# A third PSUM bank for the exponential scores: the step sums go through the work ring, and x's transpositions move to slots 8 to 11

## The chip, the cores and the metric

The kernel runs on one core of one Trainium2 chip. The metric is the device time of one execution in microseconds; the time given for a kernel is the median of its runs.

## What is computed

x is (16, 512, 512) in float32: 16 batches of 512 tokens with 512 features. The reference runs two attention layers one after the other, and the change touches the first only. With the masks all ones it computes, for each batch and each of H = 16 heads of 32 features:

```
xn  = layer_norm(x, norm_w, norm_b)
q   = (xn @ q_w + q_b).reshape(B, T, H, -1)
k   = (xn @ k_w + k_b).reshape(B, T, H, -1)
att = softmax(einsum('bnhl,bmhl->bnmh', q, k) + (1 - mask) * -1e6, axis=2)
v   = ((xn @ v_w + v_b) * src_mask[:, :, None]).reshape(B, T, H, -1)
y   = einsum('bnmh,bmhl->bnhl', att, v).reshape(B, T, D)
e   = silu(cond) @ emb_w + emb_b          # scale and shift, from the condition
h   = silu(layer_norm(y, ...) * (1 + scale) + shift) @ out_w + out_b
x   = x + h
```

The second layer is an efficient-attention block with 8 heads, of the same sizes.

## The kernel before

The program has two phases. `attention_phase` computes q, k, v, the softmax numerators and y of the first layer for all batches, and leaves y and the softmax sums in DRAM. `projection_phase` does the rest. Only `attention_phase` changes.

**Steps and slots.** A batch b is done in NG = 4 steps g, and a step handles a group of HG = 4 heads. A step has SLOTS = 16 slots, k = 0 to 15, written out by hand in the program of each engine. In the slots of step (b, g), TensorE (PE) does four kinds of work:

- *Exponential scores* (`exp_scores`, L521 [PE]): one 512-column matmul each, 16 in a step, called e0 to e15 here. They lag by LAG = 3 slots: slot k computes exponential score k - 3 of this step (slots 0 to 2 do e13 to e15 of the step before). ScalarE (ACT) turns each into `probs` (`exp`, L745). There are two `exp_bank`s, so score e must wait until ACT has read score e - 2.
- *Maximum scores* (`max_scores`, L506): the same scores of the next step, transposed, m0 to m15, one and a half in a slot, in slots 0 to 10. Even slots have one; odd slots have two, with a quarter of a projection between them. VectorE (DVE) takes the row maxima (`maximum`, L879) from two `max_bank`s: score m waits until maximum m - 2 is done.
- *Bursts*: in the slot of e6 (slot 9) `weigh_values` of the previous step's key tiles 2 and 3 (L532, 16 records), then `sum_probs` (L546), which sums `probs_sum` over the keys; in the slot of e8 (slot 11) `weigh_values` of this step's key tiles 0 and 1. `probs_sum` is added up by GpSimd (POOL, `add_probs`, L284, three adds of 128x2048 in a step); the last batch's last step does it on DVE.
- *Work through the ring* of two `work_bank`s, taken in turn in a fixed order (`uses_of`): the projections of q in slots 0 to 3 and of k in slots 4 to 7 for two steps ahead (L489, three matmuls in a quarter, one quarter in a slot), two tiles of v in steps 0 and 3 in slots 8 to 11 and 13 to 15, the turned maxima `m` in slot 12 (`transpose_max`, L512), and in step 1 the four transpositions of x of the next batch (`transpose_x`, L496) in slots 8, 9, 11 and 13. A use takes its bank when the use two before it has been read (`take_bank`). For q and k the bank is read by ACT (`high_of`, L719) and then by DVE (`low_of`, L865). For x it is ACT `high_of_x` (L713) and DVE `low_of_x` (L860), the latter one slot later. For v it is DVE `add_value_bias` (L874) in slot 11 or 15. For m it is DVE `split_shift` (L890, L892), which SP then sends by two DMAs (`shift_rows`, L333) into the rows that e0 of the next step needs.

ACT also issues the DMAs of the high parts of q and k behind `high_of` (`stack_high`, L726), copies y (`copy_y`, L752) at e6, and in step 0 copies the sums of the batch before (`copy_sums`, L758) at e8. DVE also normalises the next x in slots 5 to 8 of step 1 (`normalise_x`, L854, a tensor_scalar from SBUF to SBUF), takes its statistics in slot 13 of step 0, and in batch 0 runs `finish_film` there (L970 to L1003).

**The sums.** `sum_probs` accumulates the four steps of a batch in one bank, `sums_bank`, which PE clears at g = 0. All eight banks are in use: 2 for maxima, 2 for exponentials, 1 for y, 1 for the sums, 2 for the ring.

## Time and profile before

| what | value |
|---|---|
| median of 3 runs | 2814.29 us (2809.64 to 2818.85) |
| time of the profiled execution | 2816.7 us |
| its span, first to last instruction | 2814.9 us |
| mean granted TensorE clock | 0.981 of full |
| attention_phase, to the last sums' store | about 1565 us |
| busy: PE, DVE, ACT, POOL | 95%, 65%, 44%, 48% |
| one full batch, in the steady state | 92.0 us |

A batch's length is read from the timeline: the same instruction (the turned maxima of step 2) starts at 708.73 us, at 800.75 us and at 892.78 us. Fifteen batches (0 to 14) have this form; batch 15 has no q, k or x of a next batch. The page gives the shares of each engine; the timeline lists instructions in order of time, with the idle time before one and what released it in brackets.

### The profile page before, as it was taken

How to read it: one execution, taken by the hardware profiler on the slowest of the kernel's cores; microseconds unless marked ns; L12 is line 12 of the kernel's file. 1: busy time of each engine (PE TensorE's matmuls, PEld its weight loads, DVE VectorE, ACT ScalarE, POOL GpSimd, SP SyncE). 2: the span in 40 equal slices, each digit the busy share in tenths (PEclk: the TensorE clock that was granted, in tenths of full speed). 3: DMA queues.
4: the chain of work that ended last, by engine and by line, in shares of the span. 5: the costliest groups of instructions: out<-in, count | busy, mean ns of one | idle time of the engine just before them, and what ended most of it. 6: DMA issues, size and time to landing. Idle time of an engine off the chain costs nothing. (4 is left out here: it accounts for less than half of the span.)

```text
span 2814.9 us, 43874 instructions
## 1 busy us (share of the span) xinstructions
PE 2676.0 (95%) x13890; PEld 1951.0 (69%) x13890; DVE 1823.3 (65%) x3276; ACT 1226.6 (44%) x2040; POOL 1343.4 (48%) x598
## 2 busy tenths in 40 slices
PE   6999999999999999999999689999999999999997
PEld 3566666656665666666664478888888888888886
DVE  4666666666666665666664666666777667766673
ACT  2455555555555555555555323333333333333332
POOL 0366656566656656665666234334333333333332
PEclk9999999999999999999998799999999999999999
DMA  7556656665666566656653411111111111111100
GB/s 182 124 96 96 101 78 97 99 100 78 97 100 99 79 96 98 95 81 94 95 80 58 147 35 50 49 49 49 49 45 49 45 40 42 41 49 44 39 30 31
DMA packets 114915, 211.44 MB, mean 75 GB/s; under 512 B 12408, under 2 KB 14508, under 8 KB 114876
## 3 DMA queue, kind: packets, MB, share of 16 engines
q1 hardware_dynamic: 78012, 143.81, 22.1%
q10 hardware_dynamic: 36864, 67.13, 17.9%
q8 instruction: 22, 0.36, 0.1%
q14 instruction: 17, 0.14, 0.0%
HBM read 74.87 MB, written 34.18 MB: 39 GB/s over the span
## 5 line engine op out<-in xcount | busy, mean ns | idle before, releaser
L879 DVE TENSOR_REDUCE negmax<-max_bank 128x1 f32<-128x512 f32 x1024 | 681.4, 687 | 311.3 <-PE max_bank L506 309.6
L745 ACT ACTIVATE probs<-exp_bank 128x512 f32<-128x512 f32 x1024 | 587.1, 596 | 530.6 <-PE exp_bank L521 494.5
L284 POOL TENSOR_TENSOR probs_sum<-probs_sum,probs 128x2048 f32<-128x2048 f32 x126 | 580.7, 4609 | 78.9 <-ACT probs L745 74.7
L284 POOL TENSOR_TENSOR probs_sum<-probs 128x2048 f32<-128x2048 f32 x63 | 287.7, 4567 | 571.3 <-ACT probs L745 571.3
L506 PE MATMUL max_bank<-k_stack,q_stack 98*128 98x512 f32 x1024 | 423.0, 417 | 22.7 <-DVE negmax L879 18.3
L521 PE MATMUL exp_bank<-q_stack,k_stack 100*128 100x512 f32 x1024 | 422.6, 424 | 22.4 <-ACT probs L745 21.7
L506 PEld LDWEIGHTS max_bank<-k_stack,q_stack 98*128 98x128 f32 x1024 | 193.7, 191 | 140.5 <-issue 58.8
L521 PEld LDWEIGHTS exp_bank<-q_stack,k_stack 100*128 100x128 f32 x1024 | 193.5, 190 | 128.1 <-ACT probs L745 72.8
L1500 POOL TENSOR_TENSOR sT_lo<-silu,sT_hi 128x512 fp32r<-128x512 f32 x128 | 172.9, 1371 | 176.4 <-DVE sT_hi L1615 176.4
L532 PE MATMUL y_bank<-probs,v_sb 128*32 128x512 f32 x2048 | 251.0, 608 | 0.0
L1281 PE MATMUL b_work<-ident,area 128*128 128x128 f32 x1536 | 192.9, 280 | 24.9 <-DMA b_sums<-sums_scratch 13.2
L1255 PE MATMUL b_work<-b_wout_hi,sT_hi 128*128 128x512 f32 x512 | 201.7, 394 | 9.6 <-issue 5.1
L1281 PEld LDWEIGHTS b_work<-ident,area 128*128 128x128 f32 x1536 | 176.1, 145 | 39.1 <-DMA b_sums<-sums_scratch 14.1
L1255 PE MATMUL b_work<-b_wout_lo,sT_hi 128*128 128x512 f32 x512 | 200.9, 392 | 0.0
L1255 PE MATMUL b_work<-b_wout_hi,sT_lo 128*128 128x512 f32 x512 | 200.9, 392 | 0.0
L1495 POOL TENSOR_TENSOR rstd_y<-var_eps_y,b_minus_half 128x4 f32<-128x4 f32 x32 | 32.7, 1022 | 333.2 <-DVE var_eps_y L1579 333.2
L1615 DVE CAST sT_hi<-silu 128x512 fp32r<-128x512 f32 x128 | 102.2, 819 | 103.8 <-ACT silu L1440 103.7
L1479 ACT ACTIVATE area<-area 128x512 f32<-128x512 f32 x64 | 40.4, 632 | 274.6 <-POOL area L1545 274.6
L1440 ACT ACTIVATE silu<-b_work,film_b,film_a 128x512 f32<-128x512 f32 x128 | 93.0, 776 | 129.0 <-PE b_work L1281 101.5
L874 DVE TENSOR_TENSOR v_sb<-work_bank,v_bias 128x512 f32<-128x512 f32 x64 | 44.2, 691 | 153.7 <-PE work_bank L489 153.7
L1515 POOL TENSOR_TENSOR result<-area,row_out 128x512 f32<-128x512 f32 x64 | 83.0, 1307 | 125.8 <-DMA out_x<-result 125.8
L532 PEld LDWEIGHTS y_bank<-probs,v_sb 128*32 128x32 f32 x2048 | 53.9, 110 | 124.0 <-issue 109.7
(203 smaller groups left out, 5294.8 us busy)
## 6 DMA issues: line engine op xcount, KB each, us to landing
q_stack<-q_stage ACTq DMA_DIRECT2D x128, 256.0 KB
k_stack<-k_stage ACTq DMA_DIRECT2D x128, 256.0 KB
x_sb<-in_x SPq DMA_DIRECT2D x16, 1024.0 KB, 5.7
q_stack<-q_stage SPq DMA_DIRECT2D x64, 256.0 KB
k_stack<-k_stage SPq DMA_DIRECT2D x64, 256.0 KB
yT_scratch<-y_stage SPq DMA_DIRECT2D x64, 256.0 KB
area<-yT_scratch SPq DMA_DIRECT2D x16, 1024.0 KB, 5.2
area<-in_x SPq DMA_DIRECT2D x64, 256.0 KB, 2.8
```

The source lines that it names most:

```text
L284: eng.tensor_tensor(probs_sum[:, :, :], so_far, probs[:, mt, :, :], ALU.add).then_inc(probs_added, 1)
L506: pe.matmul(max_bank[m % 2][:, :], q_stack[0:ROWS_MAX, g, j, nt * P:(nt + 1) * P], k_stack[0:ROWS_MAX, g, j, :], start=True, stop=True).th ...
L521: pe.matmul(exp_bank[k % 2][:, :], k_stack[0:ROWS_EXP, g, j, mt * P:(mt + 1) * P], q_stack[0:ROWS_EXP, g, j, :], start=True, stop=True).th ...
L532: last = pe.matmul(y_bank[DH0 * j:DH0 * (j + 1), :], v_sb[:, mt, P * j + DH0 * g:P * j + DH0 * (g + 1)], probs[:, mt, j, :], start=(mt == ...
L745: act.activation(probs[:, mt, j, :], exp_bank[k % 2][:, :], ACT.Exp).then_inc(exp_done, 1)
L879: dve.tensor_reduce(negmax[:, m:m + 1], max_bank[m % 2][:, :], AXX, ALU.max, negate=True).then_inc(max_done, 1)
L1255: last = pe.matmul(out, lhs(a, kt), rhs(c, kt), start=(kt == 0 and a + c == 0), stop=(kt == KT - 1 and a == 1))
L1281: last = pe.transpose(out[:, i * P:(i + 1) * P], src(i), ident[:, :])
L1440: act.activation(silu[:, kt % SILUS, :], bank(u), ACT.Silu, scale=film_columns(film_a[film], kt, row), bias=film_columns(film_b[film], kt, ...
L1500: pool.tensor_tensor(sT_lo[:, kt, :], silu[:, kt % SILUS, :], sT_hi[:, kt, :].bitcast(F32), ALU.subtract).then_inc(sT_lo_done, 1)
L1515: pool.tensor_tensor(result[:, tt, :], x_sb[:, tt, :], rows["out1"][:, :], ALU.add).then_inc(result_biased, 1)
L1615: dve.tensor_copy(sT_hi[:, kt, :], silu[:, kt % SILUS, :]).then_inc(sT_hi_done, 1)
```

## The change

- `sums_bank` goes. Its PSUM bank becomes `exp_bank[2]`. Exponential score e uses bank e mod 3, except e15, which uses bank 1. So e2 to e14 wait for the reading of e - 3 (e2: e14 of the step before), e15 waits for e13, e1 waits for e15 of the step before, and e0 for e12 of the step before.
- `sum_probs` of every step takes a bank of the ring, as a use `s` in slot 9, and no longer accumulates. DVE adds each step's sum into `sums_stage` in SBUF (`gather_sums`, slot 9): a copy at g = 0, an add at the other steps. ACT's `copy_sums` goes.
- The first tile of v takes its quarters in slots 9, 10, 10, 11. x is transposed in slots 8, 9, 10 and 11, so all before `m`. The ring's order in step 1 was q, k, x0, x1, x2, m, x3; it becomes q, k, x0, s, x1, x2, x3, m. In steps 0 and 3 it was q, k, v, m, v'; it becomes q, k, s, v, m, v'. A batch has 24 uses where it had 20.
- DVE takes only the first maximum of a slot at the slot's start; the second comes at the slot's end, behind the slot's other DVE work.
- `finish_film` moves from slot 13 to slot 4 of the very first step. The film products use `exp_bank[2]` and `y_bank` in place of `sums_bank`.

```diff
@@ -169,9 +169,8 @@
         minus_half = sb("minus_half", [P, TT])
 
         max_bank = [bank(f"max_bank{i}") for i in range(2)]
-        exp_bank = [bank(f"exp_bank{i}") for i in range(2)]
+        exp_bank = [bank(f"exp_bank{i}") for i in range(3)]
         y_bank = bank("y_bank")
-        sums_bank = bank("sums_bank")
         work_bank = [bank(f"work_bank{i}") for i in range(2)]
 
...
         def uses_of(g, last):
-            u = []
+            at = []
             if not last or g < NG - 2:
-                u += ["q", "k"]
-            if g == 0:
-                u += ["v2"]
+                at += [(QUARTERS[n][0], n) for n in "qk"]
+            if g == 0 or (g == NG - 1 and not last):
+                mt = 2 if g == 0 else 0
+                at += [(QUARTERS["v"][0], f"v{mt}"), (QUARTERS["v'"][0], f"v{mt + 1}")]
             if g == 1 and not last:
-                u += [f"x{tt}" for tt in range(TT - 1)]
-            if g == NG - 1 and not last:
-                u += ["v0"]
+                at += [(k, f"x{tt}") for tt, k in enumerate(X_TURNS)]
             if not last or g < NG - 1:
-                u += ["m"]
-            if g == 1 and not last:
-                u += [f"x{TT - 1}"]
-            if g == 0:
-                u += ["v3"]
-            if g == NG - 1 and not last:
-                u += ["v1"]
-            return u
+                at.append((MAX_TURN, "m"))
+            return [n for _, n in sorted(at + [(LAG + FIRST_BURST, "s")])]
+
+        QUARTERS = {"q": (0, 1, 2, 3), "k": (4, 5, 6, 7), "v": (9, 10, 10, 11), "v'": (13, 14, 15, 15)}
+        X_TURNS = (8, 9, 10, 11)
+        MAX_TURN = 12
+        FIRST_BURST = 6
+        SECOND_BURST = 8
 
         FIRST_USES = [f"x{tt}" for tt in range(TT)] + ["q0", "k0", "q1", "k1", "m", "v0", "v1"]
         USES = sum(len(uses_of(g, False)) for g in range(NG))
         assert USES % 2 == 0
 
 
-        QUARTERS = {"q": (0, 1, 2, 3), "k": (4, 5, 6, 7), "v": (8, 9, 10, 11), "v'": (13, 14, 15, 15)}
-        X_TURNS = (8, 9, 11, 13)
-        MAX_TURN = 12
-
...
         def use(b, g, what, last=False):
 
-            n = len(FIRST_USES) + sum(len(uses_of(h, last)) for h in range(g)) + uses_of(g, last).index(what)
+            uses = uses_of(g, last)
+            n = len(FIRST_USES) - 1 + sum(len(uses_of(h, last)) for h in range(g)) + uses.index(what)
+            if type(b) is int and b == 0 and g == 0 and uses.index(what) < uses.index("s"):
+                n += 1
             return n, b * USES + n
+
+        def final_use():
+
+            n = len(FIRST_USES) - 1 + sum(len(uses_of(h, True)) for h in range(NG))
+            return n, (B - 1) * USES + n
+
+        def exp_bank_of(k):
+            return exp_bank[1 if k == SLOTS - 1 else k % 3]
+
+        def exps_in_front(s, k):
+
+            if k < 3:
+                return SLOTS * (s - 1) + (13, 16, 15)[k]
+            return SLOTS * s + (k - 1 if k == SLOTS - 1 else k - 2)
 
...
-        def add_probs(eng, s, mt, first=False):
+        def add_probs(eng, s, mt, sums_use=None):
 
             eng.wait_ge(exp_done, SLOTS * s + HG * (mt + 1))
             if mt == 1:
-                if not first:
-
-                    eng.wait_ge(sums_full, s)
+                if sums_use is not None:
+
+                    eng.wait_ge(work_full, sums_use + 1)
                 so_far = probs[:, 0, :, :]
...
                     pe.wait_ge(shift_in[g], 2 * DMA * (b + 1))
-                if not (first and k < 2):
-                    pe.wait_ge(exp_done, SLOTS * step_of(b, g) + k - 1)
-                pe.matmul(exp_bank[k % 2][:, :], k_stack[0:ROWS_EXP, g, j, mt * P:(mt + 1) * P],
+                if not (first and k < 3):
+                    pe.wait_ge(exp_done, exps_in_front(step_of(b, g), k))
+                pe.matmul(exp_bank_of(k)[:, :], k_stack[0:ROWS_EXP, g, j, mt * P:(mt + 1) * P],
                           q_stack[0:ROWS_EXP, g, j, :], start=True, stop=True).then_inc(exp_full, 1)
...
                     pe.wait_ge(y_read, s)
+                if type(s) is int and s == 0:
+                    pe.wait_ge(film_step, 2)
...
-            def sum_probs(b, g):
-
-                s = step_of(b, g)
-                pe.wait_ge(probs_added, (TT - 1) * (s + 1))
-                if type(s) is int and s == 0:
-                    pe.wait_ge(film_step, 2)
-                if g == 0 and not (type(b) is int and b == 0):
-                    pe.wait_ge(sums_read, b)
+            def sum_probs(b, g, number):
+
+                out = take_bank(number)
+                pe.wait_ge(probs_added, (TT - 1) * (step_of(b, g) + 1))
                 for j in range(HG):
-                    last = pe.matmul(sums_bank[DH0 * j:DH0 * (j + 1), :], head_sel[:, g, :],
-                                     probs_sum[:, j, :], start=(g == 0), stop=(g == NG - 1))
-                last.then_inc(sums_full, 1)
+                    last = pe.matmul(out[DH0 * j:DH0 * (j + 1), :], head_sel[:, g, :],
+                                     probs_sum[:, j, :], start=True, stop=True)
+                last.then_inc(work_full, 1)
...
-                if e == 6 and not first:
+                if e == FIRST_BURST and not first:
                     weigh_values(*before, 2)
                     weigh_values(*before, 3)
-                    sum_probs(*before)
-                if e == 8:
+                    sum_probs(*before, use(b, g, "s", last))
+                if e == SECOND_BURST:
                     weigh_values(b, g, 0)
                     weigh_values(b, g, 1)
...
-            def copy_sums(b):
-                act.wait_ge(sums_full, NG * (b + 1))
-                if not (type(b) is int and b == 0):
-                    act.wait_ge(sums_stored, DMA * HG * b)
-                act.activation(sums_stage[:, :], sums_bank[:, :], ACT.Copy).then_inc(sums_read, 1)
...
-                if e == 8 and g == 0 and not first:
-                    copy_sums(b - 1)
...
+            def gather_sums(b, g, sums_use, sums_use_in_front):
+
+                static, number = sums_use
+                dve.wait_ge(work_full, number + 1)
+                if g == 0:
+                    if not (type(b) is int and b == 0):
+                        dve.wait_ge(sums_stored, DMA * HG * b)
+                    done = dve.tensor_copy(sums_stage[:, :], work_bank[static % 2][:, :])
+                else:
+                    dve.wait_ge(work_read, sums_use_in_front + 1)
+                    done = dve.tensor_tensor(sums_stage[:, :], work_bank[static % 2][:, :], sums_stage[:, :], ALU.add)
+                done.then_inc(work_read, 1)
...
                     if has_next:
-                        for m in maxima(k):
+                        for m in maxima(k)[:1]:
                             maximum(n_b, n_g, m)
...
+                    if k == LAG + FIRST_BURST and not (type(b) is int and b == 0 and g == 0):
+                        before = (b, g - 1) if g else (b - 1, NG - 1)
+                        in_front = None if g == 1 else use(b, g - 1, "s", last)[1] if g else use(b - 1, NG - 1, "s")[1]
+                        gather_sums(*before, use(b, g, "s", last), in_front)
...
                     if g == 0 and not last and k == 13:
                         statistics_of_x(b + 1)
-                        if type(b) is int and b == 0:
-                            finish_film()
+                    if type(b) is int and b == 0 and g == 0 and k == 4:
+                        finish_film()
+                    if has_next:
+                        for m in maxima(k)[1:]:
+                            maximum(n_b, n_g, m)
...
-                add_probs(dve, step_of(B - 1, NG - 1), mt)
+                add_probs(dve, step_of(B - 1, NG - 1), mt, use(B - 1, NG - 1, "s", True)[1])
+            gather_sums(B - 1, NG - 1, final_use(), use(B - 1, NG - 1, "s", True)[1])
```

## Rows read from the trace of the kernel before

**Rows 1.** The page, busy time of the engines.

```profile
PE 2676.0 (95%) x13890; PEld 1951.0 (69%) x13890; DVE 1823.3 (65%) x3276; ACT 1226.6 (44%) x2040; POOL 1343.4 (48%) x598
```

**Rows 2.** Waits, us in total, times, longest, 100 to 1600 us.

```profile
PEld exp_bank L521 <- ACT probs L745: 72.5, 144, 1.2
...
PE exp_bank L521 <- ACT probs L745: 21.7, 54, 0.8
...
PE work_bank L496 <- DVE xT_lo L860: 12.7, 15, 0.9
```

**Rows 3.** Timeline of PE, end of step 2 (start, length, instruction, idle before).

```profile
800.78 0.48 PE L521 MATMUL exp_bank<-q_stack,k_stack 100*128 100x512 f32 x1
801.60 0.98 PE L521 MATMUL exp_bank<-q_stack,k_stack 100*128 100x512 f32 x2 [0.34 <-ACT probs L745]
802.78 0.50 PE L521 MATMUL exp_bank<-q_stack,k_stack 100*128 100x512 f32 x1 [0.21 <-ACT probs L745]
```

**Rows 4.** Timeline of ACT, the same stretch.

```profile
800.95 2.97 ACT L745 ACTIVATE probs<-exp_bank 128x512 f32<-128x512 f32 x5 [1.54 <-PE exp_bank L521]
```

**Rows 5.** Timeline of PE and its weight loads around e3, slot 6 of step 2.

```profile
882.13 0.39 PE L506 MATMUL max_bank<-k_stack,q_stack 98*128 98x512 f32 x1
...
882.45 0.19 PEld L521 LDWEIGHTS exp_bank<-q_stack,k_stack 100*128 100x128 f32 x1 [0.36 <-ACT probs L745]
```

**Rows 6.** Timeline of DVE, slots 5 to 8 of step 1.

```profile
859.04 1.39 DVE L879 TENSOR_REDUCE negmax<-max_bank 128x1 f32<-128x512 f32 x2
860.35 0.97 DVE L854 TENSOR_SCALAR x_sb<-x_sb,mv,rstd 128x512 f32<-128x512 f32 x1
...
861.84 0.53 DVE L854 TENSOR_SCALAR x_sb<-x_sb,mv,rstd 128x512 f32<-128x512 f32 x1
```

**Rows 7.** Timeline of POOL, the same stretch.

```profile
856.43 4.61 POOL L284 TENSOR_TENSOR probs_sum<-probs_sum,probs 128x2048 f32<-128x2048 f32 x1
```

**Rows 8.** Timeline of PE, slots 8 to 15 of step 1.

```profile
863.03 0.50 PE L506 MATMUL max_bank<-k_stack,q_stack 98*128 98x512 f32 x1 [0.31 <-DVE negmax L879]
...
866.85 0.50 PE L506 MATMUL max_bank<-k_stack,q_stack 98*128 98x512 f32 x1
...
870.64 0.66 PE L496 MATMUL work_bank<-ident,x_sb 128*128 128x128 f32 x4
...
872.72 0.66 PE L496 MATMUL work_bank<-ident,x_sb 128*128 128x128 f32 x4 [0.84 <-DVE xT_lo L860]
...
874.55 0.50 PE L521 MATMUL exp_bank<-q_stack,k_stack 100*128 100x512 f32 x1 [0.71 <-ACT probs L745]
```

**Rows 9.** Timeline of DVE and ACT, slots 9 to 12 of step 1.

```profile
867.38 1.36 DVE L879 TENSOR_REDUCE negmax<-max_bank 128x1 f32<-128x512 f32 x2 [1.64 <-PE max_bank L506]
868.66 0.68 DVE L860 TENSOR_TENSOR xT_lo<-work_bank,xT_hi 128x512 fp32r<-128x512 f32 x1
...
871.34 0.60 ACT L713 ACTIVATE xT_hi<-work_bank 128x512 fp32r<-128x512 f32 x1 [1.69 <-PE work_bank L496]
871.83 1.08 ACT L745 ACTIVATE probs<-exp_bank 128x512 f32<-128x512 f32 x2
```

**Rows 10.** Timeline around finish_film in batch 0: DVE, POOL, PE.

```profile
109.75 3.21 DVE L995 TENSOR_SCALAR film_a<-film_a 128x64 f32<-128x64 f32 x2
...
108.16 4.60 POOL L284 TENSOR_TENSOR probs_sum<-probs_sum,probs 128x2048 f32<-128x2048 f32 x1 [1.34 <-ACT probs L745]
...
115.28 0.49 PE L506 MATMUL max_bank<-k_stack,q_stack 98*128 98x512 f32 x1 [3.17 <-DVE negmax L879]
```

**Rows 11.** Stretch by stretch: us, busy (count) of PE, PEld, DVE, ACT, POOL, granted clock, DMA, GB/s.

```profile
803.10:812.50 9.40, 9.40 (x41) 7.40 (x41) 7.28 (x11) 4.99 (x9) 9.03 (x2) 1.00 0.69 175
110.00:120.00 10.00, 6.68 (x21) 4.77 (x21) 7.82 (x14) 2.89 (x5) 6.83 (x4) 0.83 0.00 0
1243.00:1247.00 4.00, 4.00 (x12) 3.18 (x13) 1.38 (x2) 1.38 (x3) 4.00 (x1) 0.60 0.03 6
```

**Rows 12.** The instructions of L333, the DMAs of the shift rows.

```profile
DMA to landing us min/median/max: 1.8/1.9/4.6
```

More of the change, by code:

```diff
@@ L382, in step @@
                 if g == 0 and not first:
-                    store_sums(b - 1)
+                    store_sums(b - 1, use(b, 0, "s", last)[1])
                 if not last or g < NG - 1:
@@ L398, in store_y, with store_sums @@
                 sp.dma_start(yT_dram[b].rearrange("(j g l) t -> g j l t", j=HG, g=NG)[g], y_stage[:, g % 2, :]).then_inc(y_stored[g % 2], DMA)
-            def store_sums(b):
-                sp.wait_ge(sums_read, b + 1)
+            def store_sums(b, sums_use):
+                sp.wait_ge(work_read, sums_use + 1)
                 for j in range(HG):
@@ L418, in _ @@
             store_y(B - 1, NG - 1)
-            store_sums(B - 1)
+            store_sums(B - 1, final_use()[1])
             for i in range(2):
@@ L445, in step @@
                     return
-                add_probs(pool, s, 1, first)
+                add_probs(pool, s, 1, None if first else use(b, g, "s", last)[1])
                 add_probs(pool, s, 2)
@@ L560, in film_products @@
                 pe.wait_ge(emb_in, DMA * 4 * (i + 1))
-                for half, out in enumerate((sums_bank, y_bank)):
+                for half, out in enumerate((exp_bank[2], y_bank)):
                     for c in range(CT // HG):
@@ L571, in film_columns @@
                 for dt in range(TE // P):
-                    last = pe.matmul((exp_bank[1], sums_bank)[i][:, dt * B:(dt + 1) * B],
+                    last = pe.matmul((exp_bank[1], y_bank)[i][:, dt * B:(dt + 1) * B],
                                      film_rows.rearrange("p h n -> p (h n)")[:, dt * P:(dt + 1) * P], row_sel[:, :],
@@ L639, in _, with exp_slot @@
             pe.wait_ge(ones_in, 2 * DMA)
-            def exp_slot(b, g, e, first=False):
+            def exp_slot(b, g, e, first=False, last=False):
                 exp_scores(b, g, e, first)
                 before = (b, g - 1) if g else (b - 1, NG - 1)
-                if e == 6 and not first:
+                if e == FIRST_BURST and not first:
                     weigh_values(*before, 2)
                     weigh_values(*before, 3)
-                    sum_probs(*before)
-                if e == 8:
+                    sum_probs(*before, use(b, g, "s", last))
+                if e == SECOND_BURST:
                     weigh_values(b, g, 0)
@@ L658, in step @@
                     if not (first and g == 0 and k < LAG):
-                        exp_slot(*exp_of(b, g, k), first and g == 0)
+                        exp_slot(*exp_of(b, g, k), first and g == 0, last)
                     if first and g == 0 and k == LAG:
@@ L705, in _ @@
             weigh_values(B - 1, NG - 1, 3)
-            sum_probs(B - 1, NG - 1)
+            sum_probs(B - 1, NG - 1, final_use())
         @block.scalar
@@ L744, in exp @@
                     act.wait_ge(probs_added, (TT - 1) * (s - 1) + max(mt, 1))
-                act.activation(probs[:, mt, j, :], exp_bank[k % 2][:, :], ACT.Exp).then_inc(exp_done, 1)
+                act.activation(probs[:, mt, j, :], exp_bank_of(k)[:, :], ACT.Exp).then_inc(exp_done, 1)
             def copy_y(b, g):
@@ L765, in copy_film @@
                 act.wait_ge(film_full, i + 1)
-                for half, src in enumerate((sums_bank, y_bank)):
+                for half, src in enumerate((exp_bank[2], y_bank)):
                     act.activation(film_rows[:, half, :], src[:, :], ACT.Copy).then_inc(film_copied, 1)
@@ L794, in exp_slot @@
                 exp(b, g, e, first)
-                if e == 6 and not first:
+                if e == FIRST_BURST and not first:
                     copy_y(*((b, g - 1) if g else (b - 1, NG - 1)))
-                if e == 8 and g == 0 and not first:
-                    copy_sums(b - 1)
             def step(b, g, last=False, first=False):
@@ L832, in _ @@
             copy_y(B - 1, NG - 1)
-            copy_sums(B - 1)
         @block.vector
@@ L968, in add_film_bias @@
                 dve.wait_ge(film_made, i + 1)
-                e = (exp_bank[1], sums_bank)[i][:, 0:2 * KT * B].rearrange("p (c b) -> p c b", b=B)
+                e = (exp_bank[1], y_bank)[i][:, 0:2 * KT * B].rearrange("p (c b) -> p c b", b=B)
                 dve.tensor_tensor(film_a[i][:, :, :], e[:, 0:KT, :], by_row(shared.eb[i][:, 0:KT]), ALU.add)
```

2 lines of the change are left out of this document (1 added, 1 removed).

## The prediction

> **What bounds the kernel now.** I read the page first. PE is busy for 95% of the span, the other engines for 44 to 65% [rows 1]. So the gain can only be idle time of PE, and the price can only be new idle time of PE. The table of waits says what that idle time is [rows 2]: PE waits for ACT to read an exponential bank (21.7 us, and its weight loads 72.5 us more, much of that hidden under a matmul that still runs), and for the low part of x (12.7 us); waits for maxima are of the same size. Then I went through the timeline of one full batch, 92.0 us, and marked each place where one matmul starts later behind the last than the usual 0.23 us (41 in 9.4 us in dense slots, a gap of 0.2 among them) [rows 11]. Four kinds of place were left that the change touches: the end of step 2, slot 6 of every step, slots 5 to 15 of step 1, and the very first step. In the dense slots (q, k, v quarters) the exponentials come 1.2 us apart, ACT needs 0.6 us for one, and a third bank has nothing to do there.
>
> **End of step 2: the third bank pays.** Slots 12 to 15 and slot 0 hold nothing but exponentials. e10 starts on PE at 800.78; e11 can't start before e9 is read and starts at 801.60; e13 waits for e11 and starts at 802.78 [rows 3]. ACT starts e9 at 800.95 and takes 2.97 us for five, 0.6 each, because it is itself fed in turn from two banks [rows 4]. Two that are both ready follow one another in 0.48 us (two in 1.08, one 0.6) [rows 9]. With three banks e11 follows e10 at once; e12 waits for e9 (read at 801.55, start 801.60); e13 waits for e10 (read at 800.95 + 0.48 + 0.60 = 802.03, start 802.10). That is 802.78 - 802.10 = 0.68 us saved. e15 and e1 still wait for the score two before, but they lie in slots 2 and 4, which are dense. Steps 0 and 3 fill slots 13 to 15 with v and have no such wait.
>
> **Slot 6.** ACT issues the two DMAs of q behind slot 3, so e1 is read late and e3 waits: its weight load 0.36 us, and the matmul starts 0.32 us after m8 instead of 0.23, and the next one 0.1 late behind it [rows 5]. In the batch that I went through, all four steps have this; the 144 waits of the weight loads [rows 2] are enough for it in all. With three banks e3 waits for e0, which is long read. That is 0.2 us a step. DVE is nearly as late there (m9 waits for maximum 7), so I take 0.18. In step 1 DVE is late anyway (below), and I take nothing. A batch gains 3 x 0.18 = 0.54.
>
> **Step 1, slots 5 to 8: the new order on DVE costs.** Before, DVE does maxima 7 and 8, then normalises the first tile of x: 0.97 us from 860.35, to 861.32, against 0.53 for the next one [rows 6]. POOL's add runs from 856.43 to 861.04 [rows 7]. The normalisation seems to stand until POOL has finished. The first step shows the same larger: two tiny operations of L995 take 3.21 us and end at 112.96, POOL's add ends at 112.76 [rows 10]. Maximum 7 starts at 859.04, and two operations of DVE follow one another in 0.6 us; the change puts the normalisation ahead of maximum 8, at about 859.64. It still ends at 861.32, and maximum 8 comes behind it, at about 861.24 to 861.92. m10 needs it; PE would be there about 1 us earlier (two slots, ten matmuls, before m12 without its wait) and starts at 861.98. DVE then has maximum 9 (to 862.5), a normalisation (to 862.97), maximum 10 (to 863.58), and m12 starts at 863.64, where it was 863.03 [rows 8]: +0.61. Two readings are to be weighed here. If the 0.97 us is a fixed cost of a first normalisation, the move costs nothing, DVE's sum up to maximum 10 is what it was, and m12 stays at 863.03. If it is a wait for POOL, it costs the 0.61. Both long rows end 0.2 to 0.3 us behind an add of POOL, so I take the wait. The Trainium skill (SBUF — State Buffer, "Who interferes with whom") says that VectorE's tensor_scalar in its two-port mode and a GpSimd instruction exclude each other for a whole instruction. By that rule the sum is the one below, and without it the sum would be 15 x 0.61 = 9 us lower; this case's rows agree with it (0.97 against 0.53).
>
> **Step 1, slots 9 to 15.** Before, x3 waits for the low part of x2 (0.84 us idle, start 872.72), and e13 for ACT (0.71, start 874.55); from m13 at 866.85 to e13 it is 7.70 us [rows 8]. In the new ring order x1 follows s, and its bank was x0's. x0's low part is computed by DVE behind maximum 13, and m13 comes behind the burst. Maximum 13 starts 0.53 after m13, the low part 0.6 later, takes 0.68 [rows 9], and x1 starts just after: m13 + 1.84, where before x1 came right behind m13, 0.33 after it. So there is 1.5 us of new idle time. m14, e7, m15, x2, e8 and the burst follow at their distances of before, in a sum of 2.0, and x3 1.85 behind the burst (no wait now: x1 was read during it): m13 + 5.69. ACT starts x3's high part 0.70 later and e9 0.49 behind that (871.34 against 870.64; 871.83) [rows 9], and reads it in 0.6, so e12 starts at x3 + 1.85 and e13, 0.48 later, at x3 + 2.33: m13 + 8.02. That is +0.32. A small wait of e6 goes (-0.08). Step 1 costs 0.61 + 0.32 - 0.08 = +0.85.
>
> **What I cost at nothing, with its cover.** The 64 gathers take DVE some 0.68 us each, by the nearest row, an operation with one PSUM and one SBUF operand [rows 9], 44 us in all. They lie behind maximum 13 and delay only maximum 14, which nobody waits for before m0 of the next step; DVE stood idle for 1.64 us before maximum 13 [rows 9]. Without that cover, 0.6 us a step or 38 us. The sum's matmuls are as many as before. The wait of s for a ring bank was met long before in steps 0, 2 and 3 (q was read in slot 4); in step 1 it needs k's low part, about 0.5 us ahead. Behind s on PE stand m13 and all maxima, so a lack there would show at once. ACT loses 16 copies of 0.6 us, out of idle time. SP sends the sums' four DMAs two slots earlier, so shift_rows has a free queue. In step 1 DVE now does x3's low part ahead of the shift: the two DMAs are issued at about 875.7 and 876.3, behind x3's low part at 875.1, and land 1.9 us later at 878.2 [rows 12]; e0 is due three dense slots behind e13 (875.4 + 3.8), its weights at 879.0. That is 0.8 us to spare; at the longest landing, 4.6, e0 would wait 1.9 us, once in a while.
>
> **First step.** finish_film now runs when POOL is idle. Before it left PE idle for 3.17 us [rows 10], and over 10 us around it the granted clock was 0.83, which is 1.7 us lost at 1.2 instead of 2.4 GHz [rows 11]. Without the wait for POOL (2.9 of the 3.21 us) some 1.7 us of small operations are left; in slot 4 they hold up m9 by about 1.5. Net -3.4 (bounds 0 and -4.9).
>
> **The sum.** Fifteen batches: 15 x (-0.68 - 0.54 + 0.85) = -5.6. Batch 15 has no x, so its step 1 ends like step 2, and has slot 6 with a DMA of q twice: -0.68 - 0.36 = -1.0. First step -3.4. Together -10.0 us: 2816.7 becomes 2806.7 for the profiled execution. That execution was 2.4 us above the median of 2814.3, so the median goes to 2804.3.
>
> **Rivals.** (a) *Likeliest, 0.43*: the sum, 2804, own range 2796 to 2811. (b) *Step 1 costs nothing, 0.22*: the normalisation doesn't stand behind POOL and x1's wait only replaces the waits of x3 and e13 that go. Then 15 x (-0.68 - 0.54 - 0.08) - 4.4 = -24: 2790. For it: two waits, 0.84 and 0.71, do go. Against it: rows 6 and 7. (c) *The exponential banks are not what slot 6 waits for, 0.20*: DVE, busy without a break there, holds m9 at the same time, and 15 x 0.54 + 0.36 = 8.5 us stay away: 2813, no change. For it: maxima and exponentials are equally late there. (d) *The clock, the other side, 0.15*: after the end of step 1, once in the trace, the granted clock falls to 0.60 over 4 us, and 1.6 us are lost [rows 11]. That was behind the waits of 0.84 and 0.71. If the new waits in step 1 (1.0 before m10, 1.5 before x1) bring this in every batch, it is +24 - 10 = +14: 2828. It decides from about 12 of the 15 batches on. Against it: the old waits did it only once in fifteen, and the new ones lie among more matmuls. The Trainium skill (TensorE: Matmul & The Clock Gate, "HAM oscillation") says that pauses between bursts of matmuls bring the array back to its lower clock; the trace agrees for that one place, and the rule gives (d) its place among the rivals.
>
> **Range and chances.** A measurement here tells about 0.3%, 8.4 us, from no change. Of (a) some six in ten lie beyond that bound. Faster 0.26 + 0.22 = 0.48; same 0.17 + 0.18 = 0.35; slower 0.15 + 0.02 = 0.17. The range from 2786 to 2823 holds (a), (c), most of (b) and the nearest part of (d).
>
> **What the changed profile would show.** Right: the idle time of PE <- ACT at the end of step 2 shrinks to about 0.3 us, no wait of a weight load before e3, a wait of about 1.5 us of x1 for xT_lo, none of x3, a normalisation of about 1.6 us in slot 5, m10 waiting for a maximum; L995 at some 0.2 us each; a batch of 91.6 us. Wrong: a normalisation of 0.53 us there (then (b)); e3 gaps still 0.32 with m9 waiting (c); a granted clock under 1 in the dense slots of step 2 (d); a wait of s or e0 that I cost at nothing.

## The result: 0.17% slower, and the profile after

The changed kernel takes 2819.69 us (median of 12 runs, 2817.21 to 2825.5), the kernel before 2814.74 us on the same chips (12 runs); the ratio is 1.0017, 95% interval 1.0009 to 1.0024. The forecast was 2804.3: the time moved the other way. It lies inside the stated range of 2786 to 2823, but that range is wide because it takes in rivals, and in the main the cause is none of them. In a later set of runs it came out the same: 2820.31 against 2815.11, ratio 1.0014 (1.0005 to 1.0023). The profiled span is 2818.6 us, 3.7 more than before.

The length of a batch says where to look. I take the distance between the same instruction in neighbouring batches (the first copy of the turned maxima, in slot 12), as the median of eight batches in the middle:

| us from slot 12 to slot 12 | step 3 to 0 | 0 to 1 | 1 to 2 | 2 to 3 | batch |
|---|---|---|---|---|---|
| before | 24.50 | 24.19 | 20.52 | 22.82 | 92.03 |
| after | 24.39 | 26.71 | 18.85 | 22.81 | 92.76 |

(The copy waits for other work of DVE in step 1, so the two middle columns are to be read together: 44.71 before, 45.56 after.) The batch was forecast 0.37 us shorter and is 0.73 longer. Step 1 costs +0.85, about as forecast (these two columns also hold slot 6 of step 2, which became 0.09 shorter, so step 1 by itself costs 0.9). What is missing is the gain of the third bank: the column that holds the end of step 2 stands at 22.81, and of slot 6 little more than 0.1 us can be seen, in the column from step 3 to step 0.

The page after: busy time of the engines, to be read beside [rows 1].

```profile
PE 2668.5 (95%) x13890; PEld 1944.4 (69%) x13890; DVE 1859.3 (66%) x3340; ACT 1201.3 (43%) x2024; POOL 1344.5 (48%) x598
```

The 64 gathers are there on DVE (its busy time rose by 36 us in all), and ACT's 16 copies are gone. The table of waits of the changed kernel, 100 to 1600 us, answers to [rows 2]:

```profile
PEld exp_bank L532 <- ACT probs L754: 36.4, 76, 0.8
...
PE work_bank L507 <- DVE xT_lo L860: 20.8, 15, 1.5
...
PE max_bank L517 <- DVE negmax L892: 18.3, 35, 1.5
...
PE max_bank L517 <- DMA k_stack<-k_stage: 7.5, 15, 0.5
PE exp_bank L532 <- ACT probs L754: 6.6, 18, 0.5
```

PE waits for ACT 15.1 us less, and its weight loads 36.1 us less. In their place stand 8.1 us more for x's low part, some 5 us more for maxima (12.9 before), and a line that the kernel before did not have among PE's waits: 15 waits of 0.5 us, one in each batch, for the rows of k.

**The end of step 2**, timeline of PE and ACT after, answering to [rows 3] and [rows 4]:

```profile
897.18 0.27 PE L523 MATMUL work_bank<-ident,negmax 128*16 128x128 f32 x1
897.21 1.81 PE L532 MATMUL exp_bank<-q_stack,k_stack 100*128 100x512 f32 x4
899.54 0.49 PE L517 MATMUL max_bank<-k_stack,q_stack 98*128 98x512 f32 x1 [0.53 <-DMA k_stack<-k_stage]
...
897.38 2.56 ACT L754 ACTIVATE probs<-exp_bank 128x512 f32<-128x512 f32 x5 [1.53 <-PE exp_bank L532]
```

The same in the kernel before:

```profile
892.78 0.28 PE L512 MATMUL work_bank<-ident,negmax 128*16 128x128 f32 x1
...
895.16 0.39 PE L506 MATMUL max_bank<-k_stack,q_stack 98*128 98x512 f32 x1
```

e10 to e13 are one run of four now, with no wait among them that the row shows: in the steady batches e13 starts 1.31 us behind e10, where it was 2.01. ACT takes 2.56 us for the five exponentials, where it took 2.97. But m0, the first maximum score of the next step, stands 0.53 us for k's rows and starts at 899.54, 2.36 us behind the turned maxima. Before, it started 2.38 us behind them. All that the third bank saves there is given back at once. m0 needs six large DMAs of 256 KB (high part of q twice, of k twice, low part of each), and they are issued in step 2 itself. The timeline of ACT's queue and of SP's shows the first and the last issue after, and the first issue before:

```profile
884.97 1.21 ACTq L735 DMA_DIRECT2D q_stack<-q_stage  x2
...
891.70 0.61 SPq L338 DMA_DIRECT2D k_stack<-k_stage  x1
```

```profile
880.48 1.21 ACTq L726 DMA_DIRECT2D q_stack<-q_stage  x2
```

and the stretch from the first issue to m0 (columns as in [rows 11]):

```profile
885.00:899.50 14.50, 13.60 (x74) 6.67 (x72) 9.00 (x16) 7.79 (x15) 8.50 (x2) 1.00 0.89 118
```

The 16 DMA engines are 89% busy in it. The last DMA is issued 7.8 us before m0 starts, while 8 KB rows land in 1.9 us [rows 12]; that it lies in a queue behind the others is a reading that an experiment below bears out. Before the change m0 started 14.68 us behind the first issue; after it, 14.57. The semaphore events of the traces have the landing itself: the last of the six lands 14.4 us behind the first issue in both kernels (median of eleven batches). Before the change m0 started 0.28 us behind that landing without waiting for it; after the change it starts 0.12 us behind it, as soon as it can. So there was room for 0.16 us and no more: the DMAs had been just hidden by e13's wait for ACT.

**Step 1**, DVE and POOL after, answering to [rows 6] and [rows 7]:

```profile
862.62 0.68 DVE L892 TENSOR_REDUCE negmax<-max_bank 128x1 f32<-128x512 f32 x1
863.22 1.65 DVE L854 TENSOR_SCALAR x_sb<-x_sb,mv,rstd 128x512 f32<-128x512 f32 x1
864.80 1.27 DVE L892 TENSOR_REDUCE negmax<-max_bank 128x1 f32<-128x512 f32 x2
...
859.98 4.62 POOL L295 TENSOR_TENSOR probs_sum<-probs_sum,probs 128x2048 f32<-128x2048 f32 x1
```

The first normalisation takes 1.65 us; it ends at 864.87, 0.27 us behind POOL's add (859.98 + 4.62 = 864.60), the same distance as before. The timeline of PE, answering to [rows 8], and of DVE, answering to [rows 9]:

```profile
865.53 0.50 PE L517 MATMUL max_bank<-k_stack,q_stack 98*128 98x512 f32 x1 [0.74 <-DVE negmax L892]
...
872.88 0.66 PE L507 MATMUL work_bank<-ident,x_sb 128*128 128x128 f32 x4 [1.38 <-DVE xT_lo L860]
...
871.54 0.69 DVE L892 TENSOR_REDUCE negmax<-max_bank 128x1 f32<-128x512 f32 x1 [1.65 <-PE max_bank L517]
872.14 0.68 DVE L860 TENSOR_TENSOR xT_lo<-work_bank,xT_hi 128x512 fp32r<-128x512 f32 x1
872.74 0.68 DVE L884 COPY sums_stage<-work_bank 128x512 f32<-128x512 f32 x1
```

m10 waits 0.74 us for maximum 8. x1 waits 1.38 us: DVE idles for 1.65 us, does maximum 13, and only then x0's low part, which x1 needs. x3 waits no more.

**The first step.** finish_film after, answering to [rows 10], and the stretches, answering to [rows 11]:

```profile
97.54 0.30 DVE L1008 TENSOR_SCALAR film_a<-film_a 128x64 f32<-128x64 f32 x2
...
99.55 0.50 PE L517 MATMUL max_bank<-k_stack,q_stack 98*128 98x512 f32 x1 [1.49 <-DVE negmax L892]
```

```profile
92.00:102.00 10.00, 8.51 (x46) 6.91 (x44) 7.09 (x19) 3.48 (x6) 0.00 (x0) 1.00 0.66 124
110.00:120.00 10.00, 9.79 (x42) 7.83 (x42) 8.46 (x20) 6.41 (x11) 7.74 (x5) 1.00 0.02 5
```

The 3.21 us have become 0.30, PE idles 1.49 us, and the granted clock is 1.00 in both places.

### The profile page after: what moved, and what is told of

Read it like the earlier page. It is cut to its first block and busy times, and to the rows that moved or that the text cites. A ratio compares the mean times of both kernels' runs of the same rounds, so it can differ in the third digit from the quotient of the medians.

```text
span 2818.6 us, 44156 instructions
## 1 busy us (share of the span) xinstructions
PE 2668.5 (95%) x13890; PEld 1944.4 (69%) x13890; DVE 1859.3 (66%) x3340; ACT 1201.3 (43%) x2024; POOL 1344.5 (48%) x598
## 3 DMA queue, kind: packets, MB, share of 16 engines
q10 hardware_dynamic: 36864, 67.13, 17.5%
## 5 line engine op out<-in xcount | busy, mean ns | idle before, releaser
L754 ACT ACTIVATE probs<-exp_bank 128x512 f32<-128x512 f32 x1024 | 573.1, 598 | 552.0 <-PE exp_bank L532 468.9
L517 PE MATMUL max_bank<-k_stack,q_stack 98*128 98x512 f32 x1024 | 430.0, 424 | 36.6 <-DVE negmax L892 23.6
L532 PE MATMUL exp_bank<-q_stack,k_stack 100*128 100x512 f32 x1024 | 411.2, 416 | 8.8 <-ACT probs L754 6.6
```

Source lines behind the costliest of these rows:

```text
L517: pe.matmul(max_bank[m % 2][:, :], q_stack[0:ROWS_MAX, g, j, nt * P:(nt + 1) * P], k_stack[0:ROWS_MAX, g, j, :], start=True, stop=True).th ...
L532: pe.matmul(exp_bank_of(k)[:, :], k_stack[0:ROWS_EXP, g, j, mt * P:(mt + 1) * P], q_stack[0:ROWS_EXP, g, j, :], start=True, stop=True).the ...
L754: act.activation(probs[:, mt, j, :], exp_bank_of(k)[:, :], ACT.Exp).then_inc(exp_done, 1)
```

## Experiments

There are eleven, and each time is the median of 4 to 12 runs of the kernel. Its ratio is to runs of the kernel before on the same chip, whose medians lie between 2815.1 and 2816.8. Where a median of the changed kernel is needed, it is 2820.3, from its own repeat. The batch lengths are read as in the table above.

### Two banks for the exponentials in the changed kernel

```diff
-            return exp_bank[1 if k == SLOTS - 1 else k % 3]
+            return exp_bank[k % 2]
...
-            if k < 3:
-                return SLOTS * (s - 1) + (13, 16, 15)[k]
-            return SLOTS * s + (k - 1 if k == SLOTS - 1 else k - 2)
+            return SLOTS * s + k - 1
...
-                if not (first and k < 3):
+                if not (first and k < 2):
```

> The changed kernel with everything in place, but the exponential scores use two banks again (score e waits for e - 2), the third stands idle. Theory A (the third bank is worth its place only where no DMA stands behind it): at the end of step 2 nothing is lost, since the first maximum score of the next step waits for the rows of k anyway; at the end of step 1 e11 to e13 come 0.6 us later, and slot 6 costs 0.1 us more in each step: 15 x (0.6 + 0.4) = +15 us over the changed kernel, 2835. Theory B (the bank pays as predicted at the end of step 2 too): 0.68 more in each batch, +25 us, 2845. Theory C (the bank is worth nothing): 2820.

2833.15 us, ratio to the kernel before 1.0062 (1.0048 to 1.0075); a batch of 93.64, 0.88 more than the changed kernel. The columns: 24.48, 26.71, 19.62, 22.83. All of the loss but 0.1 is in the column of the end of step 1 (1 to 2, +0.77); in that of the end of step 2 it is 0.02. Theory A, with 0.88 us where it had 1.0. The bank is worth 0.9 us a batch, and nothing at the place for which I had priced it highest. Without it the wait of m0 for the rows of k is gone from the table of PE's waits: it is hidden again.

### DVE's order of before, but for slot 9

```diff
-                        for m in maxima(k)[:1]:
+                        for m in maxima(k)[:1] if k == 9 else maxima(k):
...
-                    if has_next:
+                    if has_next and k == 9:
                         for m in maxima(k)[1:]:
```

> The changed kernel with DVE's order of before in slots 0 to 8 and 10 (both maxima first, then the normalisation); slot 9 keeps the new order. Theory A (the normalisation stands behind POOL's add and carries maximum 8 with it): it takes 0.9 to 1.0 us again instead of 1.65, m10 waits no more, m12 waits 0.3 as before; 0.6 to 0.7 us less in each of 15 batches, -10 us against the changed kernel, 2810. Theory B (the long normalisation is a fixed cost of the first one, wherever it stands): no change, 2820.

2809.07 us, ratio 0.9973 (0.9964 to 0.9982); a batch of 92.13, 0.63 less than the changed kernel. DVE in slots 5 and 6 of step 1, and POOL beside it:

```profile
855.54 1.40 DVE L892 TENSOR_REDUCE negmax<-max_bank 128x1 f32<-128x512 f32 x2
856.86 0.96 DVE L854 TENSOR_SCALAR x_sb<-x_sb,mv,rstd 128x512 f32<-128x512 f32 x1
...
852.92 4.61 POOL L295 TENSOR_TENSOR probs_sum<-probs_sum,probs 128x2048 f32<-128x2048 f32 x1
```

The same instruction takes 1.65 us at one place and 0.96 at the other, and what stays is its end, 0.29 us behind POOL's add here (857.82 and 857.53). A fixed cost would not do that. Theory A.

### The low part of x0 ahead of maximum 13

```diff
+                    if g == 1 and not last and k == 9:
+                        low_of_x(0, use(b, 1, "x0")[0], high_count(b, 1, 2))
                     if has_next:
                         for m in maxima(k)[:1]:
                             maximum(n_b, n_g, m)
...
-                    if g == 1 and not last and k - 1 in X_TURNS:
+                    if g == 1 and not last and k - 1 in X_TURNS[1:]:
```

> The changed kernel with the low part of x0 ahead of maximum 13 on DVE in slot 9 of step 1, in the time in which DVE stands idle for 1.65 us. Theory A (x1's wait is one for the place of this operation in DVE's order): x1's idle time of 1.38 us goes, x2 waits some 0.3 us for the gathered sum, e13 comes about 1.2 us earlier; 15 x 1.2 = -18 us, 2802. Theory B (the time is bound by ACT's and DVE's work on the four tiles, and comes back as waits of x2, x3 or e12): less than -5 us, 2815 to 2820.

2800.13 us, ratio 0.9945 (0.9932 to 0.9959); a batch of 91.59, 1.17 less than the changed kernel, where 1.2 was expected. DVE and PE in slots 9 and 10 of step 1:

```profile
860.55 0.69 DVE L860 TENSOR_TENSOR xT_lo<-work_bank,xT_hi 128x512 fp32r<-128x512 f32 x1
862.15 0.69 DVE L892 TENSOR_REDUCE negmax<-max_bank 128x1 f32<-128x512 f32 x1 [0.91 <-PE max_bank L517]
862.75 0.68 DVE L884 COPY sums_stage<-work_bank 128x512 f32<-128x512 f32 x1
...
861.61 0.50 PE L517 MATMUL max_bank<-k_stack,q_stack 98*128 98x512 f32 x1
861.95 0.60 PE L507 MATMUL work_bank<-ident,x_sb 128*128 128x128 f32 x4
```

x1 is back right behind m13 (0.34 us). DVE does the low part in its idle time, which shrinks from 1.65 to 0.91. Theory A.

### One of the six DMAs made small, after the change and before it

```diff
-                    act.dma_start(stack_rows(what, row, g), stage[what][:, 0, :].bitcast(F32)).then_inc(stack_in[g], DMA)
+                    dst, src = stack_rows(what, row, g), stage[what][:, 0, :].bitcast(F32)
+                    if part and what == "q" and row == 2:
+                        dst, src = dst[:, 0, :], src[0:DH0, :]
+                    act.dma_start(dst, src).then_inc(stack_in[g], DMA)
```

`part` is true from batch 1 on.

> The changed kernel, in which one of the six large DMAs of a step's q and k rows (the second copy of q's high part) carries only one of the four heads from batch 1 on; the other heads keep the rows of an earlier batch, so this leaves out part of the data. Theory A (from slot 3 of step 2 on the six DMAs, one behind the other, set when m0 of the next step can start): the wait of m0 for the k rows, 0.53 us, goes, and e13 sets the start again; with it the 0.68 us of the third bank is seen: 0.5 to 0.8 us in 14 batches, -7 to -11 us, 2810. Theory B (m0's wait only hides another one, of ACT or DVE): no change, 2820.

> The kernel before, with the same shortened DMA (the second copy of q's high part carries one of four heads from batch 1 on, so part of the data is left out). Theory A (before the change, the rows of k had landed just when e13, held up by ACT, was through: the DMAs were hidden, and so was what they would do to a third bank): no change, 2816. Theory B (the DMAs slow other work down in either kernel, and the gain of the changed kernel with the short DMA was not that of m0's wait): -8 to -12 us here too, 2806.

After the change: 2804.11 us, ratio 0.9958 (0.9944 to 0.9971); a batch of 91.95, 0.81 less, of which 0.78 is in the column from step 2 to step 3 (22.03). Before the change: 2815.56 us, ratio 1.0001 (0.9991 to 1.0012), a batch of 92.07. The end of step 2 with the small DMA, after the change:

```profile
890.21 0.27 PE L523 MATMUL work_bank<-ident,negmax 128*16 128x128 f32 x1
890.24 1.81 PE L532 MATMUL exp_bank<-q_stack,k_stack 100*128 100x512 f32 x4
891.88 0.40 PE L517 MATMUL max_bank<-k_stack,q_stack 98*128 98x512 f32 x1
```

m0 starts 1.67 us behind the turned maxima, 0.69 sooner than with all six DMAs in full. That is the 0.68 us that the prediction had worked out for the third bank. The last landing comes 1.0 us sooner in both kernels (13.4 us behind the first issue). The same shortening is worth nothing before the change, so the DMAs are not slowing other work down. Theory A in both. The median fell by 16 us where 14 to 15 batches of 0.81 are some 12. In the profiled executions the largest other difference lies in one place, from slot 12 of step 1 to slot 12 of step 2 in batch 15, where PE has no projections: the changed kernel takes 22.0 us for it, this one 16.8, and the stretches show why. First the changed kernel's, then this one's:

```profile
1523.00:1545.00 22.00, 20.85 (x75) 8.38 (x73) 11.86 (x20) 9.74 (x18) 13.66 (x4) 0.69 0.10 25
```

```profile
1510.00:1527.00 17.00, 15.90 (x76) 6.21 (x74) 11.43 (x19) 9.60 (x17) 13.89 (x4) 1.00 0.09 26
```

The granted clock is 0.69 in one and 1.00 in the other. The kernel before with the small DMA has the short form too (17.5 us, where the kernel before has 21.8), and its median is no lower. The changed kernel itself has 22.0 in one profile and 20.9 in the other. So this is not shown to be an effect of the DMA; what sets it stays open.

### Both mends of step 1 together

The two edits above in one kernel.

> The changed kernel with both mends of step 1: DVE's order of before in slots 0 to 8 and 10, and the low part of x0 ahead of maximum 13 in slot 9. Theory A (two separate costs): their gains add up, 0.63 + 1.17 = 1.8 us in each of 15 batches, a batch of 90.96 us, -27 us against the changed kernel, about 2793. Theory B (one hides the other, as with the DMAs at the end of step 2): a batch of 91.4 or more, 2800.

2795.62 us, ratio 0.9933 (0.9919 to 0.9947); a batch of 91.03, 1.73 less than the changed kernel against 1.80 for the sum of the two. Two separate costs. This kernel, with the third bank and both mends, has a batch 1.0 us shorter than the kernel before.

### The first tile of v one slot earlier

```diff
-        QUARTERS = {..., "v": (9, 10, 10, 11), "v'": (13, 14, 15, 15)}
+        QUARTERS = {..., "v": (9, 9, 10, 10), "v'": (13, 14, 15, 15)}
```

> The kernel of the run before it, with the four quarters of the first tile of v in slots 9, 9, 10, 10 in place of 9, 10, 10, 11, so that DVE reads v's bank during the second burst. Theory A (the second tile of v waits in slot 13 only for that reading): the idle time of 0.33 us, with its start 0.57 us late, goes in steps 3 and 0, about 1.0 us in a batch, -15 us against the run before it. Theory B (e10 or the turned maxima hold slot 13 up at the same time): less than 0.3 us in a batch, -4 us.

2776.93 us, ratio 0.987 (0.9853 to 0.9887), the fastest kernel here: 1.3% under the kernel before, and 18.7 us under the one without this edit, where 15 x 0.86 are 13. Its profile has the short form of the stretch in batch 15 (17.9 us against 22.0). A batch of 90.17, 0.86 less than without this edit, in the columns 3 to 0 (23.92) and 2 to 3 (22.44). The wait for v (9.8 us, 31 times, both in the kernel before and in the changed one) is gone. That it is faster by more than its batches may lie in that stretch; this is not shown. In its table of PE's waits the rows of k stand with 7.4 us, much the same as the 7.5 of the changed kernel:

```profile
PE max_bank L517 <- DVE negmax L892: 12.4, 36, 1.5
PE max_bank L517 <- DMA k_stack<-k_stage: 7.4, 15, 0.6
```

### finish_film alone, in the kernel before

```diff
                     if g == 0 and not last and k == 13:
                         statistics_of_x(b + 1)
-                        if type(b) is int and b == 0:
-                            finish_film()
+                    if type(b) is int and b == 0 and g == 0 and k == 4:
+                        finish_film()
```

> The kernel before with nothing but finish_film moved from slot 13 to slot 4 of the first step. Theory A (its 3.21 us were a wait for POOL's add, and the lower clock came of PE's idle time): L995 takes 0.3 us, PE stands idle for about 1.5 us instead of 3.2, the granted clock stays at 1.00; -3 us, 2813.5. Theory B (first use of this code is what takes 3 us): no change, L995 stays long.

2810.75 us, ratio 0.9986 (0.9976 to 0.9996): -4.6 us in the medians, with an interval of about -1 to -7; expected -3. The profile agrees better: from the copy of the first turned maxima to slot 12 of step 2 in batch 0 it takes 77.7 us in place of 79.5, with a fall of the granted clock in it that costs 1.5, so 3.3 us are gained. In its timeline of DVE:

```profile
95.86 0.30 DVE L995 TENSOR_SCALAR film_a<-film_a 128x64 f32<-128x64 f32 x2
```

POOL does nothing between 92 and 102 us there. The idle time of PE is 1.31 us, the granted clock 1.00. Theory A: first use of the code costs nothing that shows.

### v one slot earlier in the kernel before

```diff
-        QUARTERS = {..., "v": (8, 9, 10, 11), "v'": (13, 14, 15, 15)}
+        QUARTERS = {..., "v": (8, 9, 10, 10), "v'": (13, 14, 15, 15)}
```

> The kernel before with the first tile of v in slots 8, 9, 10, 10 in place of 8 to 11, and nothing else. Theory A (the wait in slot 13 has nothing to do with the third bank): steps 3 and 0 become 0.4 to 0.5 us shorter each, 0.9 us in a batch, -13 us, 2802. Theory B (with two exponential banks the two projection quarters in slot 10 hold e8 up, or ACT gives the gain back): less than half of that, 2810.

2811.48 us, ratio 0.9986 (0.9977 to 0.9995). The batch is 91.26, 0.77 shorter, as theory A has it, but the median fell by 3.6 us in place of 12. Neither theory has the reason. Five of the fifteen batches have the column from step 1 to 2 longer by 1.5 us (22.05 to 22.13 where the others have 20.5). Four us of one of them, behind the end of step 1, and two of the matmuls in it:

```profile
876.00:880.00 4.00, 4.00 (x11) 3.10 (x11) 1.39 (x2) 1.42 (x3) 4.00 (x1) 0.57 0.02 6
...
877.27 0.63 PE L489 MATMUL work_bank<-xT_hi,wq_lo 128*128 128x512 f32 x1
877.69 0.63 PE L521 MATMUL exp_bank<-q_stack,k_stack 100*128 100x512 f32 x1
```

The granted clock is 0.57: for most of this stretch the array runs at 1.2 GHz, and the matmuls in it start 0.42 us behind one another, where it is 0.23 at 2.4 GHz. The kernel before has one such batch, so this edit brings four more, 6 us of the 0.77 x 15 = 11.6. Another 1.0 us goes in the step of finish_film in batch 0 (30.2 us in place of 29.2). What is left, 4.4 us, is near the 4.8 by which the profiled spans differ and the 3.6 of the medians. It is no matter of one execution: the mean granted clock is 0.976 to 0.979 in all eleven runs of this kernel, and 0.979 to 0.982 in the 21 runs of the kernel before beside it.

### Two banks in the fastest kernel, and the changed kernel again

The edit of the first experiment in the kernel with both mends and v earlier; and the changed kernel itself.

> The fastest kernel so far (both mends of step 1, v one slot earlier) with two exponential banks in use and the third idle: what the third bank is worth once the rest is mended. Theory A (as in the first run of two banks: the end of step 1 and slot 6, nothing at the end of step 2): 0.9 to 1.0 us in a batch, +15 us, 2792. Theory B (with x1's wait gone, the bank matters more at the end of step 1): 1.5 or more in a batch, 2800. Theory C (nothing): 2777.

> The changed kernel once more, on the same chip as these runs. All theories: 2819 to 2822, a batch of 92.76 us.

2795.47 us, ratio 0.9927 (0.9913 to 0.994), a batch of 91.14: 18.5 us and 0.97 us a batch more than with three banks (15 x 0.97 = 14.6). Theory A in the batch. The wait for the rows of k is gone from the table of PE's waits here too. The changed kernel: 2820.31, a batch of 92.76.

## Why the prediction was wrong

**The step that failed is the end of step 2.** The prediction worked out that e13 starts 0.68 us sooner, and put these 0.68 us into the sum 15 times, 10 us in all. e13 does start sooner, by 0.70. What stands behind e13 on PE, m0 of the next step, was not followed to what it waits for. The prediction followed the shift rows to e0 (there was room, and still is), but not the six DMAs of q and k to m0. Step 2 is the shortest step, and the last of these DMAs lands 14.4 us behind the first issue. e13's wait for ACT had hidden them with 0.16 us to spare. The pair of runs with the small DMA shows it: 0.78 us in that column after the change, nothing before. The question "where a stall goes, what is late next" has its answer here, and I asked it only of one of the two queues.

**Slot 6** is the term that was mis-sized: forecast at 0.18 us in three steps, 0.54 in all, it brought 0.1 net. PE and its weight loads there, after:

```profile
886.63 0.40 PE L517 MATMUL max_bank<-k_stack,q_stack 98*128 98x512 f32 x1
886.86 0.40 PE L532 MATMUL exp_bank<-q_stack,k_stack 100*128 100x512 f32 x1
887.10 0.49 PE L517 MATMUL max_bank<-k_stack,q_stack 98*128 98x512 f32 x1
...
887.09 0.19 PEld L517 LDWEIGHTS max_bank<-k_stack,q_stack 98*128 98x128 f32 x1 [0.27 <-DVE negmax L892]
```

e3 follows m8 by 0.23 us and m9 follows e3 by 0.24, so m9 does come 0.19 us sooner (it was 0.32 and 0.34). But now the weight load of m9 waits for DVE, and m10 comes 1.26 us behind m9 in place of 1.17: half is lost at once. That DVE is the next limit there had been rival (c), and about half of it is true. What is left, 0.1 us, can be seen whole in step 0 alone. In step 2 it lies ahead of the wait for the DMAs, which swallows it. In step 3, m8 comes 7.33 us behind m0 in place of 7.25 (with the small DMA it is 7.25 again), and the column shows nothing.

These two terms make up the miss in a batch. The forecast was -0.37 and the result +0.73, 1.10 more: 0.67 of the 0.68 at the end of step 2 and 0.43 of the 0.54 in slot 6.

**Step 1** was right in its mechanisms and nearly in its size: +0.85 forecast, +0.85 measured in the two columns, 0.9 without the 0.09 of slot 6 that they hold. Of its parts, the normalisation was forecast at 0.61 and is 0.63 (second run); x1's idle time was forecast at 1.5 and is 1.38; what was called a wait for POOL rather than a fixed cost is one (0.96 and 1.65 us for the same instruction, each ending 0.27 to 0.29 us behind the add). The Trainium skill's rule (SBUF — State Buffer, "Who interferes with whom") agrees with all three rows: the instruction is held up to the end of POOL's, and not slowed by a factor. That the instruction is in the two-port mode that the rule speaks of is shown by no run here.

**The first step** was right for this edit alone: 3.4 us forecast, 4.6 measured in the medians, with the forecast within the interval, and 3.3 in the profile. In the changed kernel less of it shows: from the first turned maxima to slot 12 of step 2 its two profiles are 0.6 and 1.8 us shorter than the kernel before, which with the 0.85 that step 1 costs makes 1.5 and 2.7. The gathers cost nothing, as said: the wait of PE for a ring bank behind a sum is not among its waits, and DVE does them beside work that nobody waits for.

**The sum** again, from the profiled executions. The marks are copies of the turned maxima, as in the table of batches.

| us | before | after |
|---|---|---|
| start to the first copy | 76.4 | 77.1 |
| to slot 12 of step 2, batch 0 | 79.5 | 78.9 |
| the next fourteen batches | 1291.1 | 1297.9 |
| to slot 12 of step 2, batch 15 | 91.0 | 90.9 |
| to the first matmul of the projection phase | 36.8 | 35.7 |
| projection phase | 1240.2 | 1238.0 |

The fourteen batches cost 6.9 us in place of 14 x 0.73 = 10.2. In the kernel before they hold a stretch of 1.5 us at the lower clock and a longer step 3 of batch 0 (23.5 us, 22.7 after); the rest is spread. The last row is no effect of the change, which does not touch that phase: in the thirteen profiles it takes between 1237.4 and 1240.3 us. The medians differ by 4.95 us, the spans by 3.7, where the forecast was -10.

Rival (d), the lower clock, did not come: the changed kernel has no such batch at all. Rival (b) is out by the second and third run. Of the cases with a chance, none was a DMA that becomes the bound. That the measured time lies within the range is luck: the range was drawn for (c) and (d), and neither is the cause.

**What the change holds.** The third bank is worth 0.9 to 1.0 us a batch in either setting, some 13 to 18 us. The change as made spends it on two places of DVE's order. Both can be mended, and the bank keeps its gain: with both mends the batch is 91.03 us, 1.0 less than before the change.

## What to carry to other kernels

When a wait is removed, name the next instruction on the same engine and follow every semaphore that it waits for back to its issue, DMAs above all: one that is hidden with 0.16 us to spare leaves no line in the table of waits. A fixed order on one engine has to be read against another's bank ring: the low part of x0 was ready, the engine was idle, and 1.2 us a batch hung on one maximum ahead of it. Where two places are mended at once, measure each alone: the gain of the bank was hidden here by two losses, each easy to take away.

## What the runs showed of the chip

The granted clock fell in some batches behind the end of step 1, always in kernels with x's transpositions in slots 8, 9, 11 and 13: in one of fifteen batches of the kernel before, in one of it with the small DMA, in two with only finish_film moved, and in five with v one slot earlier (0.57 over 4 us, 1.5 us lost each). There it fell in none of the nine profiles with the transpositions in slots 8 to 11, two of them with two banks. The end of step 1 has idle times of PE of 0.84 and 0.71 us close to one another, and little work between. The kernel with a batch shorter by 0.77 us and the same idle times had more of these falls, which is one case and no rule. That the idle times cause them was not tried by itself, and why it is some batches and not others stays open; an experiment for it would have to vary these idle times alone. Batch 15 adds its own: between 16.8 and 22.0 us for the same stretch of the program, with a granted clock of 1.00 in the shortest and 0.69 in the longest. So an edit that takes time out elsewhere can give half of it back in this way (6 of 11.6 us). The distances between equal instructions, batch by batch, show it; in the page's row of the clock, where a slice is 70 us, four of the five falls lie in slices that stand at 9, and the mean clock of the run falls by 0.003 only (0.978 against 0.981).
